# VectorE sums the first half of the value products before it scales the normalised rows; TensorE moves two products between a flip and its use

## The chip, the cores and the metric

One NeuronCore of one Trainium2 chip. The metric is the time of the whole program on the device, in microseconds (us). The engines are TensorE (PE; PEld is its weight load), VectorE (DVE), ScalarE (ACT), GpSimd (POOL) and SyncE (SP, which only issues DMAs). Each runs its own instruction list in order, and they meet at semaphores.

## The reference

2048 rows of 256 values (4 sequences of 512) pass two gated blocks. The first block is the part that the change touches. With `ln` a layer norm:

```python
x = x + tanh(g_xattn[0]) * L0_xattn(ln(x), ctx)      # attention inside a row
x = x + tanh(g_ffn[0])   * L0_ffn(ln(x))             # shared expert + one of 8 experts
x = x + tanh(g_xattn[1]) * L1_xattn(ctx, ctx, ln(x)) # attention over the sequence
x = x + tanh(g_ffn[1])   * L1_ffn(ln(x))             # expand, butterflies, gelu, contract

# L0_xattn, for one row: Q, K, V are 16 heads of 16 values
qk = einsum('ih,jh->ij', Q, K) / 4        # i, j index the 16 values, h the heads
valued = einsum('ij,jh->ih', softmax(qk), V)
out = valued.reshape(256) @ Wo.T
# shared expert
y = (gelu(x @ w1s) * (x @ w2s)) @ w3s
```

Each row attends only to itself, so `qk` and `valued` are 4096 products a row each. They can't be done as matmuls; VectorE and GpSimd do them element by element.

## The kernel before

The first part handles 16 tiles of 128 rows in a software pipeline. A step works on up to five tiles: `t0` (newest) has its keys, values and queries projected, `t1` its scores computed, `t2` its attention finished, `t3` its output projected, normalised and sent into the shared expert, `t4` its shared expert finished. Step number t has `t0 = t`; so tile n is `t1` in step n + 1 and `t3` in step n + 3. Steps 0 to 5 and 16 are written out, steps 6 to 15 run as a loop of two steps (an even and an odd one), and a `drain` finishes the last three tiles. Every engine has its own `step` function, so the order in which each takes the tiles is written by hand.

On VectorE a step starts with `scores` (L1540, 4096 products of queries in PSUM with keys) and `score_sums` (L1549), with `mult` (L1738, the two halves of gelu times up) ahead of each. Then come short ones: `add_attended` (L1559), the layer norm of `t3` (`stats` L1564, `moments` L1569, `guarded` L1574), row maximum and shift of `t1` (L1588, L1597), `guarded_first` (L1582), `exp_sums` (L1605), `shares` (L1621). `normal_rows` (L1615) scales the 128x256 rows of `t3`; it needs the reciprocal root that GpSimd makes from `guarded`. `attended` sums the value products in two halves (L1630, twice) and scales them (L1638). `add_shared` (L1646) adds the shared expert's rows.

GpSimd in a step: `second_root` of `t3` (L552), then for `t1` twice a product of 2048 (L619, in and out of SBUF) and an add of its halves (L621), with `first_root` (L559) between. There is one buffer, PRODV, of two halves:

```python
gp.wait_ge(s["exp_done"], n + 1)
gp.wait_ge(s["kv_sb"], n + 1)
for hf in range(2):
    gp.wait_ge(s["av_read"], 2 * (n - 1) + hf + 1)
```

So the first product of a tile waits until the exponentials are there (ACT L1277) and VectorE has summed the same half of the tile before.

TensorE in a step: flip of the attended rows (PB[3]), `out_rows`, second half of the up products of `t4`, keys and values of `t0` (128x512), its queries (128x256), `down_rows`, flip of the normalised rows, `gate`, first half of the up products of `t3`. Between a flip and its use ScalarE copies the turned rows from PSUM (L1217, L1222). ScalarE also loads its function table again whenever it turns from gelu to exponential and back (ACT_TABLE_LOAD).

SyncE loads tile t + 2 into the buffers of tile t once `kv_done` and `q_done` of tile t are there, after it has stored the normalised rows of `t3` (`keep_rows`).

Of the kernel before, what the change touches and what calls it, by code (L numbers as in the profile page):

```python
# [23 lines left out]
ALU = mybir.AluOpType  # L24
ACT = mybir.ActivationFunctionType
AX = mybir.AxisListType
# [6 lines left out]
NH = 16  # L33
# [21 lines left out]
def build(nc, x, xT, ctxT, gates, wq0, wkv0, wo0, wg, wexp, wk1, wv1, wq1, wo1, bo1,  # L55
          weT, uplow, dnlow, high, cols, wc, bc, db, out):
    with ExitStack() as ctx:
# [323 lines left out]
        def first(jp, n):  # L381
            return isinstance(jp[0], int) and num(jp) < n
# [346 lines left out]
        def _(pe):  # L729
# [30 lines left out]
            def up_half(t3, hf):  # L760

                n = 2 * num(t3) + hf
                for bank, w, done, free in ((PB[6], W1, "h1_done", "gelu_done"),
                                            (PB[7], W2, "h2_done", "mult_done")):
                    if not (first(t3, 1) and hf == 0):
                        pe.wait_ge(s[free], n)
                    for q in range(4):
                        m = 4 * hf + q
                        product(bank[:, q * P:(q + 1) * P], lambda k: w[:, k, m * P:(m + 1) * P],
                                lambda k: X2T[:, t3[1], k, :], KD, s[done] if q == 3 else None)  # L770
# [12 lines left out]
            def out_rows(t3):  # L783

                n3 = num(t3)
                pe.wait_ge(s["aT_sb"], n3 + 1)
                if not first(t3, 1):
                    pe.wait_ge(s["lg_sb"], n3)
                product(PB[5][:, 0:D], lambda k: AT[:, k, :], lambda k: WO0[:, k, :], KD, s["o_done"])
# [9 lines left out]
            def normal_rows(t3):  # L799

                pe.wait_ge(s["xn2_ready"], num(t3) + 1)
                flip(PB[3], XH[:, t3[1], :], s["x2T_done"])
# [6 lines left out]
            def step(of):  # L809
                t0, t3, t4 = of(0), of(3), of(4)  # L810
                if t3 is not None:
                    attended(t3)
                    out_rows(t3)
                if t4 is not None:
                    up_half(t4, 1)
                if t0 is not None and first(t0, 1):
                    warm(PB[0], 8)
                    pe.wait_ge(exact, 2)
                    pe.wait_ge(wq_in, 16)
                    product(PB[5][:, 0:D], lambda k: rounded(ONES[:, :]), lambda k: WQ0[:, k, :], KD,  # L820
                            s["wq_mean"])
                    pe.wait_ge(s["wq_ready"], 1)
                    queries(t0)
                    pe.wait_ge(w_in, 16)
                if t0 is not None:
                    n = num(t0)
                    pe.wait_ge(tile_in[t0[1]], 48 * t0[0] + 48)
                    if not first(t0, 1):
                        pe.wait_ge(s["kv_sb"], n)
                    product(PB[4][:, :], lambda k: CTX[:, t0[1], k, :], lambda k: WKV0[:, k, :], KD,  # L830
                            s["kv_done"])
                    if not first(t0, 1):
                        queries(t0)
                    if first(t0, 2) and not first(t0, 1):
                        pair_products()
                if t4 is not None:
                    down_rows(t4)
                if t3 is not None:
                    normal_rows(t3)
                if t3 is not None:  # L840
                    gate(t3)
                    up_half(t3, 0)
                if t0 is not None and first(t0, 2) and not first(t0, 1):
                    fold_up()
# [6 lines left out]
            def queries(t0):  # L851

                pe.wait_ge(tile_in[t0[1]], 48 * t0[0] + 48)
                if not first(t0, 1):
                    pe.wait_ge(s["qk_prod"], num(t0))
                product(PB[1][:, 0:D], lambda k: XT[t0[1]][:, k, :], lambda k: WQ0[:, k, :], KD, s["q_done"])
# [670 lines left out]
        def _(dve):  # L1527
# [18 lines left out]
            def score_sums(t1):  # L1546

                dve.wait_ge(s["qk_prod"], num(t1) + 1)
                dve.tensor_reduce(SCP.rearrange("p (i j) -> p i j", i=DK),  # L1549
                                  PRODQ[:, :].rearrange("p (i j h) -> p i j h", i=DK, j=DK), AX.X, ALU.add)\  # L1550
                    .then_inc(s["scores"], 1)

            def add_attended(t3):

                n3 = num(t3)
                dve.wait_ge(s["o_done"], n3 + 1)
                if first(t3, 1):
                    dve.wait_ge(tanh_s, 1)
                dve.scalar_tensor_tensor(X[:, n3, :], PB[5][:, 0:D], TG[:, 0:1], X[:, n3, :],  # L1559
                                         ALU.mult, ALU.add).then_inc(s["x1_ready"], 1)  # L1560
# [24 lines left out]
            def row_max(t1):  # L1585

                dve.wait_ge(s["scores"], num(t1) + 1)
                dve.tensor_reduce(SM[:, 0, :], SCP.rearrange("p (i j) -> p i j", i=DK), AX.X, ALU.max)\  # L1588
                    .then_inc(s["rowmax"], 1)
# [28 lines left out]
            def shares(t2):  # L1618

                dve.wait_ge(s["sums"], num(t2) + 1)  # L1620
                dve.reciprocal(RI[:, :], SM[:, 1, :]).then_inc(s["recip"], 1)  # L1621

            def attended(t2):

                n2 = num(t2)
                aov = AOP.rearrange("p (i h) -> p i h", i=DK)
                H2 = NH // 2
                for hf in range(2):
                    dve.wait_ge(s["av_half"], 2 * n2 + hf + 1)
                    dve.tensor_reduce(  # L1630
                        aov[:, :, hf * H2:(hf + 1) * H2],
                        PRODV[:, :].rearrange("p (f i h j) -> p f i h j", f=2, i=DK, h=H2)
                        [:, hf, :, :, 0:DK // 2], AX.X, ALU.add).then_inc(s["av_read"], 1)
                dve.wait_ge(s["av_read"], 2 * n2 + 2)
                dve.wait_ge(s["recip"], n2 + 1)
                if not first(t2, 1):
                    dve.wait_ge(s["aT_done"], n2)
                dve.tensor_tensor(AO[:, :].rearrange("p (i h) -> p i h", i=DK), aov,  # L1638
                                  spread(RI[:, :].rearrange("p (i o) -> p i o", o=1), 2, NH),
                                  ALU.mult).then_inc(s["a_ready"], 1)  # L1640

# [7 lines left out]
            def step(of):  # L1649
                t0, t1, t2, t3, t4 = of(0), of(1), of(2), of(3), of(4)  # L1650
                if t1 is not None:
                    scores(t1)
                if t4 is not None:
                    mult(t4, 0)
                if t1 is not None:
                    score_sums(t1)
                if t4 is not None:
                    mult(t4, 1)
                if t3 is not None:
                    add_attended(t3)  # L1660
                if t3 is not None:
                    hold(s["x1_ready"], num(t3) + 1)
                    stats(t3, 1, "ln2")
                if t1 is not None:
                    row_max(t1)
                if t3 is not None:
                    moments(t3, 1, "ln2")
                if t1 is not None:
                    shift(t1)
                if t3 is not None:  # L1670
                    guarded(t3, 1, "ln2")
                if t0 is not None:
                    guarded_first(t0)
                if t2 is not None:
                    exp_sums(t2)
                    shares(t2)
                if t3 is not None:
                    normal_rows(t3)
                if t2 is not None:
                    attended(t2)  # L1680
                if t4 is not None:
                    add_shared(t4)

            def second_norm(t3):

# [6 lines left out]
            def drain():  # L1692

                a, b, c = tile(T - 3), tile(T - 2), tile(T - 1)
                mult(a, 0)
                second_norm(b)
                exp_sums(c)
                shares(c)
                normal_rows(b)
                mult(a, 1)  # L1700
                attended(c)
                add_shared(a)
                mult(b, 0)
                second_norm(c)
                normal_rows(c)
                mult(b, 1)
                choices()
                add_shared(b)
                places()
                mult(c, 0)  # L1710
                one_hots()
                mult(c, 1)
                expert_of_tiles()
                inverse()
                slots_of_tiles()
                add_shared(c)
# [494 lines left out]
```

## Time and profile before

| | |
|---|---|
| median of 3 runs | 770.26 us (768.25 to 772.27) |
| profiled execution | 768.17 us, span 766.4 us |
| busy share | PE 91%, DVE 79%, POOL 54%, ACT 50% |
| granted TensorE clock, mean | 0.98 |
| first part | about 0 to 297 us |
| the 16 score products on VectorE | first starts 12.3 us, last 257.3 us |

Times in rows are in microseconds from the start of the span unless marked ns. A line number is that of the kernel before. "Idle before" is the time for which the engine stood still ahead of the instruction, with what released it.

### The profile page before, as it was taken

The numbers are of one execution on the slowest core, as the hardware profiler recorded it, in microseconds if no ns is written. First come the engines' busy times: TensorE is split into PE (matmuls) and PEld (weight loads), VectorE is DVE, ScalarE is ACT, GpSimd is POOL, SyncE is SP. The second block draws the span as 40 slices with busy tenths as digits, with TensorE's granted clock in tenths as the row PEclk, the third lists the DMA queues.
The fourth block names the chain that finished last, engine by engine and source line by source line (L and its number), as shares of the span: only waits on it lengthen the run. The fifth ranks groups of instructions, "written<-read, shape, count | busy, mean of one in ns | idle before, by whom it ended". The sixth has DMA issues, their size and how long they took to land.

```text
span 766.4 us, 12694 instructions
## 1 busy us (share of the span) xinstructions
PE 697.5 (91%) x4347; PEld 585.7 (76%) x4347; DVE 607.5 (79%) x910; ACT 380.2 (50%) x682; POOL 416.6 (54%) x304
## 2 busy tenths in 40 slices
PE   6659999999999899889999999999976999999996
PEld 4438888878887788567777777777865999989996
DVE  4789999999999945799978887887787767677653
ACT  2323433433433321366666777666643575555643
POOL 3898888888889880406987666665032101110000
PEclk9959999999999999999999999999998999999999
DMA  9501010011036012232354416000010101000000
GB/s 285 202 28 29 28 29 27 27 34 48 28 97 289 8 62 69 69 138 97 123 193 189 189 29 248 28 22 21 15 36 27 35 21 56 29 28 8 15 15 21
DMA packets 28642, 56.43 MB, mean 74 GB/s; under 512 B 3408, under 2 KB 24656, under 8 KB 27440
## 3 DMA queue, kind: packets, MB, share of 16 engines
q1 hardware_dynamic: 23408, 47.64, 17.4%
q0 software_dynamic: 1872, 5.11, 2.5%
q10 hardware_dynamic: 3312, 3.02, 1.2%
q8 instruction: 30, 0.49, 0.3%
q14 instruction: 20, 0.16, 0.1%
HBM read 48.55 MB, written 7.21 MB: 73 GB/s over the span
## 4 chain that ended last, share of the span: by engine, by line
PE 50%; DVE 19%; POOL 12%; issue 10%; ACT 7%; DMA 1%; DVEq 1%; POOLq 0%; ACTq 0%
PE bank L733 20%; PE bank L742 16%; POOL PRODV L619 8%; PE bank L988 8%; PE bank L750 4%; DVE PRODQ L1540 2%; POOL PRODV L621 2%; DVE SLOT_r L1917 2%; DVE bank L1549 2%; DVE PRODV_r L1917 2%; DVE bank L1630 2%; DVE STC L2005 1%; ACT L1446 1%; ACT XS L1446 1%; ACT L1277 1%
## 5 line engine op out<-in xcount | busy, mean ns | idle before, releaser
L619 POOL TENSOR_TENSOR PRODV<-SHARED 128x2048 f32<-128x2048 f32 x32 | 144.7, 4522 | 28.8 <-DVE bank L1630 25.0
L733 PE MATMUL bank<-ROWS,SLOT 128*128 128x128 f32 x1024 | 122.8, 279 | 0.0
L733 PEld LDWEIGHTS bank<-ROWS,SLOT 128*128 128x128 f32 x1024 | 120.4, 195 | 0.8
L712 POOL TENSOR_TENSOR RS<-VE,MHALF 128x2 f32<-128x2 f32 x16 | 13.1, 819 | 151.1 <-DVE VE L2012 151.1
L733 PE MATMUL bank<-SLOT,XST 128*128 (+1 forms) x184 | 82.9, 593 | 0.5 <-ACT XST L1344 0.5
L621 POOL TENSOR_TENSOR PRODV<-PRODV 128x1024 f32<-128x1024 f32 x32 | 74.7, 2335 | 2.5
L1549 DVE TENSOR_REDUCE bank<-PRODQ 128x256 f32<-128x4096 f32 x16 | 70.7, 4419 | 0.1
L1540 DVE TENSOR_TENSOR PRODQ<-bank,SHARED 128x4096 f32<-128x4096 f32 x16 | 70.6, 4413 | 0.0
L636 POOL DMA_INDIRECT XS<-normal_rows,INV x23 | 27.4, 1192 | 71.2 <-PE bank L750 49.9
L1917 DVE TENSOR_TENSOR PRODQ_r<-SLOT,ROWS_r 128x1024 fp32r<-128x1024 f32 x44 | 63.6, 1446 | 0.0
L733 PE MATMUL bank<-SLOT,HA 128*128 128x256 f32 x256 | 58.3, 381 | 2.4 <-DVE HA L1738 2.4
L1917 DVE TENSOR_TENSOR SHARED_r<-bank,HA_r 128x512 fp32r<-128x512 f32 x46 | 31.5, 686 | 35.8 <-ACT HA_r L1338 35.2
L733 PEld LDWEIGHTS bank<-SLOT,XST 128*128 128x128 f32 x184 | 33.2, 190 | 33.8 <-issue 33.0
L1917 DVE TENSOR_TENSOR W_r<-SLOT,PRODQ_r 128x1024 fp32r<-128x1024 f32 x44 | 57.6, 1308 | 0.0
L1331 ACT ACTIVATE PRODQ_r<-SLOT 128x1024 fp32r (+1 forms) x44 | 46.5, 1057 | 21.1 <-issue 20.6
L733 PEld LDWEIGHTS bank<-SLOT,HA 128*128 128x128 f32 x256 | 48.1, 190 | 9.3 <-DVE HA L1738 2.9
L1354 ACT ACTIVATE ROWS_r<-SLOT 128x1024 fp32r (+1 forms) x46 | 49.2, 1071 | 6.4 <-PE bank L742 6.4
L988 PE MATMUL bank<-W_r,HA_r 128*128 128x256 f32 x176 | 49.6, 282 | 0.0
L988 PE MATMUL bank<-PRODQ_r,SHARED_r 128*128 128x256 f32 x176 | 49.5, 281 | 0.0
L988 PE MATMUL bank<-PRODQ_r,HA_r 128*128 128x256 f32 x176 | 49.5, 281 | 0.0
L742 PE MATMUL bank<-ROWS_r,WORK_r 128*128 128x512 f32 x136 | 48.9, 399 | 0.0
L742 PE MATMUL bank<-SLOT_r,PRODQ_r 128*128 128x256 f32 x256 | 47.6, 286 | 1.4 <-DVE SLOT_r L1917 1.4
(269 smaller groups left out, 1828.1 us busy)
## 6 DMA issues: line engine op xcount, KB each, us to landing
SLOT<-wexp SPq DMA_DIRECT2D x9, 3072.0 KB, 11.5
ROWS<-xT SPq DMA_DIRECT2D x16, 128.0 KB, 2.2
SHARED<-ctxT SPq DMA_DIRECT2D x16, 128.0 KB, 2.4
X<-x SPq DMA_DIRECT2D x16, 128.0 KB, 2.4
normal_rows<-ROWS SPq DMA_DIRECT2D x16, 128.0 KB, 1.7
WET<-ctxT SPq DMA_DIRECT2D x4, 512.0 KB, 8.4
out<-X SPq DMA_DIRECT2D x16, 128.0 KB, 1.7
expert_rows<-YS ACTq DMA_DIRECT2D x12, 128.0 KB, 1.7
```

The costliest lines, as they stand in the source:

```text
L619: gp.tensor_tensor(o, pr, v, ALU.mult).then_inc(s["av_prod"], 1)
L621: gp.tensor_tensor(o[:, :, :, 0:DK // 2], o[:, :, :, 0:DK // 2], o[:, :, :, DK // 2:DK], ALU.add).then_inc(s["av_half"], 1)
L636: gp.indirect_dma_start(out=XS[:, n % 2, :], out_offset=None, in_=xs, in_offset=bass.IndirectOffsetOnAxis(ap=INV[:, n:n + 1], axis=0))\
L733: last = pe.matmul(dst, lhs(k), rhs(k), start=(k == 0), stop=(k == chunks - 1))
L742: last = pe.matmul(dst, f32r(a), f32r(b), start=(k == 0 and n == 0), stop=(k == chunks - 1 and n == 2))
L750: last = pe.transpose(bank[:, k * P:(k + 1) * P], src[:, k * P:(k + 1) * P], IDENT[:, :])
L988: last = pe.matmul(PB[7][:, 0:D], f32r(a[:, k, :]), f32r(b[:, k, :]), start=(k == 0 and i == 0), stop=(k == KF - 1 and i == 2))
L1331: act.activation(f32r(w3h[:, 4 * r:4 * r + 4, :].rearrange("p k d -> p (k d)")), slot_part(held_for[n2], 2 * KD * F + r * 4 * D, 4 * D), A ...
L1354: act.activation(f32r(W2H[:, :, hf * 512:(hf + 1) * 512]), up_part(held_for[n], hf), ACT.Copy)\
L1540: dve.tensor_tensor(PRODQ[:, :].rearrange("p (i j h) -> p i j h", i=DK, j=DK), spread(PB[1][:, 0:D].rearrange("p (i o h) -> p i o h", i=DK ...
L1549: dve.tensor_reduce(SCP.rearrange("p (i j) -> p i j", i=DK), PRODQ[:, :].rearrange("p (i j h) -> p i j h", i=DK, j=DK), AX.X, ALU.add)\
L1917: dve.tensor_tensor(f32r(lo), value, rounded(high), ALU.subtract).then_inc(done, 1)
```

## The change

On VectorE the two sums of value products leave `attended` and become `value_sums(t2, hf)`. The first is put after `guarded(t3)` and ahead of `normal_rows(t3)`, the second right after it. `shares`, `add_shared` and what is left of `attended` (one product) follow in this order. `add_attended` goes ahead of the second `mult`, `guarded_first` ahead of `moments`, and `exp_sums` ahead of `guarded`. In `drain` both sums stand directly before `attended`, where they were.

On TensorE `out_rows` goes behind the second half of the up products, and `queries` goes from behind keys and values to the place between the flip of the normalised rows and `gate`.

```diff
@@ TensorE, step
                 if t3 is not None:
                     attended(t3)
-                    out_rows(t3)
                 if t4 is not None:
                     up_half(t4, 1)
+                if t3 is not None:
+                    out_rows(t3)
...
-                    if not first(t0, 1):
-                        queries(t0)
                     if first(t0, 2) and not first(t0, 1):
                         pair_products()
                 if t4 is not None:
                     down_rows(t4)
                 if t3 is not None:
                     normal_rows(t3)
+                if t0 is not None and not first(t0, 1):
+                    queries(t0)
                 if t3 is not None:
                     gate(t3)
                     up_half(t3, 0)
@@ VectorE
+            def value_sums(t2, hf):
+                H2 = NH // 2
+                dve.wait_ge(s["av_half"], 2 * num(t2) + hf + 1)
+                dve.tensor_reduce(
+                    AOV[:, :, hf * H2:(hf + 1) * H2],
+                    PRODV[:, :].rearrange("p (f i h j) -> p f i h j", f=2, i=DK, h=H2)
+                    [:, hf, :, :, 0:DK // 2], AX.X, ALU.add).then_inc(s["av_read"], 1)
@@ VectorE, step
                 if t1 is not None:
                     score_sums(t1)
+                if t3 is not None:
+                    add_attended(t3)
                 if t4 is not None:
                     mult(t4, 1)
-                if t3 is not None:
-                    add_attended(t3)
                 if t3 is not None:
                     hold(s["x1_ready"], num(t3) + 1)
                     stats(t3, 1, "ln2")
                 if t1 is not None:
                     row_max(t1)
+                if t0 is not None:
+                    guarded_first(t0)
                 if t3 is not None:
                     moments(t3, 1, "ln2")
                 if t1 is not None:
                     shift(t1)
+                if t2 is not None:
+                    exp_sums(t2)
                 if t3 is not None:
                     guarded(t3, 1, "ln2")
-                if t0 is not None:
-                    guarded_first(t0)
                 if t2 is not None:
-                    exp_sums(t2)
-                    shares(t2)
+                    value_sums(t2, 0)
                 if t3 is not None:
                     normal_rows(t3)
                 if t2 is not None:
-                    attended(t2)
+                    value_sums(t2, 1)
+                    shares(t2)
                 if t4 is not None:
                     add_shared(t4)
+                if t2 is not None:
+                    attended(t2)
```

## Rows read from the trace of the kernel before

**Rows 1.** Costliest groups of the page: busy and mean ns, idle before, releaser.
```profile
L619 POOL TENSOR_TENSOR PRODV<-SHARED 128x2048 f32<-128x2048 f32 x32 | 144.7, 4522 | 28.8 <-DVE bank L1630 25.0
```

**Rows 2.** Timeline of POOL, steps 11 and 12: start, us, instruction, idle before.
```profile
186.46 0.54 POOL L552 TENSOR_TENSOR MV<-MV,MHALF 128x1 f32<-128x1 f32 x1
188.84 4.53 POOL L619 TENSOR_TENSOR PRODV<-SHARED 128x2048 f32<-128x2048 f32 x1 [1.84 <-DVE bank L1630]
...
195.75 0.55 POOL L559 TENSOR_TENSOR ROW<-ROW,MHALF 128x1 f32<-128x1 f32 x1
196.27 4.53 POOL L619 TENSOR_TENSOR PRODV<-SHARED 128x2048 f32<-128x2048 f32 x1
...
203.18 0.55 POOL L552 TENSOR_TENSOR MV<-MV,MHALF 128x1 f32<-128x1 f32 x1
205.49 4.54 POOL L619 TENSOR_TENSOR PRODV<-SHARED 128x2048 f32<-128x2048 f32 x1 [1.76 <-DVE bank L1630]
```

**Rows 3.** Timeline of DVE over the same steps.
```profile
187.22 0.41 DVE L1615 TENSOR_SCALAR ROWS<-X,MV 128x256 f32 x1 [0.84 <-POOL MV L552]
...
190.26 0.48 DVE L1646 SCALAR_TENSOR_TENSOR X<-bank,TG,X 128x256 f32 x1
190.66 4.41 DVE L1540 TENSOR_TENSOR PRODQ<-bank,SHARED 128x4096 f32<-128x4096 f32 x1
...
200.51 0.47 DVE L1559 SCALAR_TENSOR_TENSOR X<-bank,TG,X 128x256 f32 x1
201.13 0.43 DVE L1564 BATCH_NORM_STATS2 ST<-X 128x6 f32 x1 [0.15 <-DVE X L1559]
...
202.01 0.43 DVE L1597 TENSOR_TENSOR ROWS<-bank,SM 128x256 f32<-128x256 f32 x1
202.35 0.14 DVE L1574 TENSOR_SCALAR MV<-MV 128x1 f32<-128x1 f32 x1
...
203.86 0.41 DVE L1615 TENSOR_SCALAR ROWS<-X,MV 128x256 f32 x1 [0.69 <-POOL MV L552]
204.19 2.35 DVE L1630 TENSOR_REDUCE bank<-PRODV 128x128 f32<-128x1024 f32 x2
```

**Rows 4.** Groups of DVE instructions by line, 90.57 to 257.33 us (ten steps).
```profile
L1615 DVE TENSOR_SCALAR ROWS<-X,MV 128x256 f32 x10 | 4.1, 413 | 7.1 <-POOL MV L552 7.1
```

**Rows 5.** Timeline of PE over the same steps.
```profile
188.06 0.38 PE L750 MATMUL bank<-IDENT,ROWS 128*128 128x128 f32 x2
188.92 0.61 PE L733 MATMUL bank<-WG,ROWS 128*128 128x8 f32 x4 [0.47 <-ACT ROWS L1222]
...
198.43 1.88 PE L733 MATMUL bank<-W,SHARED 128*128 128x512 f32 x4
...
204.47 0.38 PE L750 MATMUL bank<-IDENT,ROWS 128*128 128x128 f32 x2
```

**Rows 6.** Timeline of ACT over the same steps.
```profile
184.11 0.60 ACT L1263 ACTIVATE SHARED<-bank 128x512 f32<-128x512 f32 x1 [3.07 <-POOL PRODV L619]
...
186.02 0.51 ACT L1277 ACTIVATE SHARED<-ROWS,ROW 128x256 f32<-128x256 f32 x1
...
203.89 0.51 ACT L1277 ACTIVATE SHARED<-ROWS,ROW 128x256 f32<-128x256 f32 x1
```

**Rows 7.** Timeline of step 3, POOL and DVE.
```profile
52.78 0.54 POOL L552 TENSOR_TENSOR MV<-MV,MHALF 128x1 f32<-128x1 f32 x1
...
53.36 0.41 DVE L1615 TENSOR_SCALAR ROWS<-X,MV 128x256 f32<-128x256 f32 x1 [1.90 <-POOL MV L552]
```

**Rows 8.** A POOL instruction of the expert part, from the timeline.
```profile
318.73 2.13 POOL L655 TENSOR_TENSOR WORK<-PRODQ,PRODV 128x1024 f32<-128x1024 f32 x1
```

**Rows 9.** One line's instructions: ns min/median/max, first and last start, forms.
```profile
L1917 DVE TENSOR_TENSOR W_r<-SLOT,ROWS_r x2: 1212/2101/2990, 319.0 to 321.9; 128x1024 fp32r<-128x1024 f32 x2
```

**Rows 10.** The same view of the two casts of L1909.
```profile
L1909 DVE CAST WK_r<-WQ x1: 414/414/414, 360.2 to 360.2; 128x512 fp32r<-128x512 f32 x1
L1909 DVE CAST WO_r<-WV x1: 859/859/859, 370.7 to 370.7; 128x512 fp32r<-128x512 f32 x1
```

More of the change, by code:

```diff
@@ L1621, in shares @@
                 dve.reciprocal(RI[:, :], SM[:, 1, :]).then_inc(s["recip"], 1)
+            AOV = AOP.rearrange("p (i h) -> p i h", i=DK)
+            def value_sums(t2, hf):
[5 more added lines that the diff above has]
+                    [:, hf, :, :, 0:DK // 2], AX.X, ALU.add).then_inc(s["av_read"], 1)
             def attended(t2):
                 n2 = num(t2)
[L1626 to L1633, printed above, removed]
                 dve.wait_ge(s["av_read"], 2 * n2 + 2)
@@ L1637, in attended @@
                     dve.wait_ge(s["aT_done"], n2)
-                dve.tensor_tensor(AO[:, :].rearrange("p (i h) -> p i h", i=DK), aov,
+                dve.tensor_tensor(AO[:, :].rearrange("p (i h) -> p i h", i=DK), AOV,
                                   spread(RI[:, :].rearrange("p (i o) -> p i o", o=1), 2, NH),
@@ L1700, in drain @@
                 mult(a, 1)
+                value_sums(c, 0)
+                value_sums(c, 1)
                 attended(c)
```

## The prediction

> **What bounds the kernel now.** I read the page first, for the costliest groups and who releases whom, then the timelines of POOL, DVE, PE and ACT over one even and one odd step of the loop, to find which loop of waits closes. The page shows that GpSimd's product of 2048 is the largest group and stood 25.0 us waiting for VectorE's sum of the value products [rows 1]. The timeline of POOL shows the loop. A step takes 205.49 - 188.84 = 16.65 us; from the score product of step 12 (190.66) to that of step 16 (257.3, in the table above) it is 66.6 / 4 = 16.66, and I use 16.67. Of it GpSimd works 203.18 + 0.55 - 188.84 = 14.89 and stands 1.76 to 1.84 [rows 2]. In that gap VectorE, which has waited 0.7 us a step for GpSimd's root [rows 4], scales the rows, sums the first half, and lets GpSimd go: 203.18 to 203.86, 204.19, 205.49 [rows 2, 3]. Though the first half of the products has been ready for 7 us, its sum stands behind an instruction that waits for GpSimd's last piece of work. PE is next: flip to flip is 16.41 us, with two stalls of 0.47 for ScalarE's copies [rows 5]. So three engines lie close: POOL 14.89, DVE 16.67 - 0.71 = 15.96, PE 16.41 - 0.94 = 15.5.
>
> **The change, VectorE.** Same instructions, another order. What shortens the list:
> - the wait for the root, 0.71 a step, if the root now comes while the first sum runs;
> - `stats` 0.62 after `add_attended`, where the next instruction could start 0.40 later, as after L1646 [rows 3]; the second mult goes between: 0.22;
> - three more waits of an instruction for the one before it (sum to reciprocal, maximum to shift, sums to scaling) get other work between; I take 0.1 each, an estimate from instructions of 256 elements, which start 0.34 apart where nothing is waited for [rows 3]. Bounds 0 and 0.45.
>
> VectorE's own loop comes to 16.67 - 0.71 - 0.22 - 0.3 = 15.44; I use 15.4.
>
> **The change, TensorE.** Each flip now has work behind it. The flip to gate distance of 0.86 [rows 5] shrinks to what two transposes take, about 0.25 (an estimate; bounds 0 and the modelled 0.38), so PE's list is 16.41 - 2 x 0.61 = 15.2, plus some 0.2 where the up products now reach the bank before the gelu has read it. `down_rows` waits for the second mult, which stands 0.4 later on VectorE; in return PE has one product less ahead. PE follows at VectorE's pace. `queries` come later, about 5 us before the next score product on the old clock and 0.3 before it on the new; slack, but little. What is moved past on SyncE's queue: loading tile t + 2 waits for these queries, some 1.5 us later, and is used a whole step later: nothing. In step 1 the pair products no longer stand behind queries that wait for VectorE, so the first exponentials come some 0.3 us earlier. In the drain PE waits 0.3 longer for the later mult of step 16. Both are estimates; they cancel.
>
> If nothing else happened: 11 steps x (16.67 - 15.4) = 14 us less.
>
> **What GpSimd now collides with.** In the kernel before, `normal_rows` (L1615) always runs while GpSimd stands still, because GpSimd's next product waits for the sum behind it [rows 2, 3]. After the change that product can start at the same moment. Does it matter? Three rows say that it does. A VectorE instruction with two SBUF inputs that takes 1.21 us took 2.99 when it started 0.3 us behind GpSimd's product of 2.13 [rows 8, 9]: it did nothing until GpSimd was through. Of two equal casts, SBUF to SBUF, one took 0.41 and one, beside GpSimd, 0.86 [rows 10]. And L1615 seems to be of the same kind as the cast: the cast does 512 elements in 0.41 us where L1597 needs 0.43 for 256, a double pace. L1615 does 256 elements with two per-row scalars in 0.41, while instructions of 256 with one such scalar take 0.47 to 0.48 at the single pace (L1559, L1646) [rows 3, 4, 10]. So it seems to run at the double pace too and, I take it, holds what GpSimd needs. The Trainium skill ("SBUF — State Buffer", Who interferes with whom) says that VectorE in a two-port mode and GpSimd hold one port pair for the whole instruction, and the second to issue blocks. By that rule the trace agrees, and the forecast below holds; without it the time would be that of the third case.
>
> The price: if GpSimd's product (4.53 us) starts first, L1615 and all behind it come up to 4.5 us late. If L1615 starts first, GpSimd loses 0.4, which it has.
>
> **Who is first.** Offsets from the start of the score product S, loop of 15.4.
> - From the shift (L1597) to the next S: 0.34 + 0.33 (sums), 0.06 (guarded), 1.13 (half of L1630), 0.33 (L1615), 1.13, 0.17 (reciprocal, estimate), 0.40, 0.34 = 4.2. So the shift is at 11.2, the first value sum at 11.9, L1615 could start at 13.0.
> - The value sum releases GpSimd 1.30 after its start (204.19 to 205.49): 13.2.
> - Even steps: the table load waits for the shift; exponentials start 1.88 after it and last 0.51 [rows 3, 6]. GpSimd's product starts at 11.2 + 1.88 + 0.51 + 0.08 = 13.65, so L1615 is first.
> - From this product to the next root are 203.18 - 188.84 = 14.34. In the following, odd, step the root starts at 13.65 + 14.34 - 15.4 = 12.6. In odd steps L1615 follows it by 187.22 - 186.46 = 0.76: 13.35. Exponentials: PE ended keys and values at 198.43 + 1.88 - 190.66 = 9.65; now `down_rows` stands directly behind them and waits for the second mult until 10.4, so they end at 10.4 to 10.6. Their copy is followed by the exponentials in 1.91 (184.11 to 186.02, the table load in between doesn't wait for the shift) [rows 6], done by 13.1. So GpSimd's product starts at 13.2, ahead of L1615 by 0.15 to 0.2. It collides: L1615 starts when the product ends, at 17.7, 4.6 later than it could, and the step lasts 20.0.
> - After it GpSimd is early, the even step is clean (15.4), and the next odd one has the same 13.65 behind it. It repeats: steps 7, 9, 11, 13, 15. Step 5 is written out, where the root is followed in 0.58, as in rows 7; it comes out just in time.
> - Step 3: GpSimd's root is last of all (52.78). A product follows a root in 0.52 (195.75 to 196.27), L1615 in 0.58 [rows 2, 7]. L1615 had waited 1.90 there, which is room for the 1.30 of the first sum, so nothing else holds GpSimd. It collides too, and PE stands behind it: +4.5, less 0.6 for PE's saved stalls: +3.9.
>
> **Sum.** +3.9 - 11 x 1.27 + 5 x 4.6 = 3.9 - 14.0 + 23.0 = +13, on the profiled 768.17 gives 781; the median shown lies 2.1 higher, and 770.26 + 13.2 = 783.5. Own range 779 to 788: loop 15.3 to 15.6, and the collision 4.4 to 4.7.
>
> **Rivals.**
> - *The odd steps are just in time, step 3 collides.* Should VectorE's tail behind the shift take 4.4 and not 4.2, the root is early enough. A step then takes about 15.55 (L1615 waits for the root): 3.9 - 11 x 1.12 = -8.4, 762. For it: every offset is good to 0.1 and the margin is 0.2. Against: a later exponential in the loop pushes the other way.
> - *No collision at all*: L1615 doesn't share with GpSimd, or wins in step 3 too. -12.3, 758. For it: no row shows L1615 beside a long GpSimd instruction. It decides from L1615 staying at 0.41 us.
> - *PE takes the wait*: mult, `down_rows`, flip and queries close a loop at 16.4 to 16.7. Then 768 to 770. Against it: 15.2 to 15.4 of work and 0.3 of slack at each crossing.
>
> **Chances.** Forecast 0.56; just in time 0.23; no collision 0.15; PE 0.06. The range takes in both signs: 757.5 to 788 leaves out about 0.15. Three runs differ by 0.5%, so 0.5% (3.9 us) is about what can be told: faster 0.39, same 0.04, slower 0.57.
>
> **What will show it.** L1615 (its new line) at 4 to 5 us in step 3 and in odd steps, with GpSimd's product running over it; even steps of 15.4 and odd ones of 20. POOL's wait for L1630 gone or 0.3. PE's stalls for L1217 and L1222 gone. If L1615 is 0.41 throughout and steps are 15.4 to 15.6, the second or third case holds. Wrong would be my offsets, if the first value sum starts more than 0.2 us earlier or later against the root than worked out.

## The result and the profile after

| | before | after |
|---|---|---|
| median | 769.31 us (4 runs, 768.25 to 772.27) | 792.43 us (4 runs, 790.45 to 793.83) |
| profiled execution | 768.17, span 766.4 | 792.09, span 790.3 |
| granted TensorE clock, mean | 0.98 | 0.955 |
| last of the 16 score products starts | 257.33 | 277.91 |
| last scaling of rows starts | 293.76 | 316.28 |

The ratio is 1.0278, with a 95% interval of 1.0258 to 1.0297: 23 us slower. The forecast was 783.5 us, slower, with an own range of 779 to 788. The direction and the collision that it named are there; the time lies above the range. The new line numbers of the changed kernel are L1541 (score products), L1616 (scaling of the rows), L1642 and L1650 (`attended`, `add_shared`), L1218 and L1223 (ScalarE's two copies) and L1278 (exponentials); L552, L619 and L1630 keep theirs.

The page of the changed kernel: the clock in 40 slices, and costliest groups.

```profile
PEclk9859998989898989989999999999999999999999
...
L619 POOL TENSOR_TENSOR PRODV<-SHARED 128x2048 f32<-128x2048 f32 x32 | 144.2, 4507 | 11.8 <-ACT SHARED L1278 10.1
...
L750 PE MATMUL bank<-IDENT,ROWS 128*128 128x128 f32 x64 | 14.4, 311 | 38.4 <-DVE ROWS L1616 31.0
```

What the change was to do it did: GpSimd's products, which stood 28.8 us, 25.0 of them for VectorE's sum [rows 1], now stand 11.8, of which 10.1 for the exponentials. The new entry is TensorE's: 31.0 us of waiting for the scaled rows, where it was 5.9 before, all in step 3. Of the 31.0, step 3 has 11.3 and five later steps 3.94 each. The view of that one line (ns min/median/max, first and last start, who waited for it):

```profile
L1616 DVE TENSOR_SCALAR ROWS<-X,MV x16: 400/408/4599, 53.4 to 316.3; 128x256 f32 x10, 128x256 f32<-128x256 f32 x6
its engine sat idle before it (us, times) until:
  POOL MV L552: 3.8, 7
who waited for it (us, times):
  PEld bank L750: 34.0, 6
  PE bank L750: 31.0, 6
```

Before, each of these took 0.41 us [rows 4]. Now ten do and six take 4.48 to 4.60: those that start at 53.41, 120.78, 158.19, 195.73, 233.27 and 270.83, in steps 3, 7, 9, 11, 13 and 15, the very ones that the forecast named. One clean odd step and one with a collision, from the timeline (start, us, instruction, idle before):

```profile
89.01 0.56 POOL L552 TENSOR_TENSOR MV<-MV,MHALF 128x1 f32<-128x1 f32 x1
89.68 0.40 DVE L1616 TENSOR_SCALAR ROWS<-X,MV 128x256 f32<-128x256 f32 x1
89.93 4.52 POOL L619 TENSOR_TENSOR PRODV<-SHARED 128x2048 f32<-128x2048 f32 x1 [0.36 <-DVE bank L1630]
...
157.42 0.55 POOL L552 TENSOR_TENSOR MV<-MV,MHALF 128x1 f32<-128x1 f32 x1
157.49 0.51 ACT L1278 ACTIVATE SHARED<-ROWS,ROW 128x256 f32<-128x256 f32 x1
158.16 4.48 POOL L619 TENSOR_TENSOR PRODV<-SHARED 128x2048 f32<-128x2048 f32 x1 [0.19 <-ACT SHARED L1278]
158.19 4.60 DVE L1616 TENSOR_SCALAR ROWS<-X,MV 128x256 f32 x1 [0.42 <-POOL MV L552]
162.71 1.22 DVE L1630 TENSOR_REDUCE bank<-PRODV 128x128 f32<-128x1024 f32 x1
...
162.85 0.69 PE L750 MATMUL bank<-IDENT,ROWS 128*128 128x128 f32 x2 [3.94 <-DVE ROWS L1616]
...
163.33 1.92 PE L733 MATMUL bank<-W,ROWS 128*128 128x256 f32 x4
...
165.75 5.33 PE L733 MATMUL bank<-ROWS,SLOT 128*128 128x128 f32 x32
```

In step 5 the scaling starts 0.25 us ahead of the product, and both run at their usual length. In step 9 the product is 0.03 ahead, and the scaling ends just behind it (162.79, against 158.16 + 4.48 = 162.64). TensorE, which waits for these rows, stands 3.94 us. Then comes what the forecast lacks: its work behind that wait is slow. The flip takes 0.69 (0.38 in [rows 5]), four products of 256 columns 1.92, 32 up products 5.33. Here are whole stretches of the changed kernel, with the granted clock in the column before the DMA share (steps 5 and 6, then 9 and 10, then the 6 us behind the collision):

```profile
76.79:92.03 15.24, 15.20 (x102) 13.23 (x101) 15.21 (x19) 6.81 (x13) 14.72 (x7) 1.00 0.12 36
92.03:107.27 15.24, 15.19 (x102) 13.26 (x101) 15.24 (x19) 6.89 (x13) 14.18 (x7) 1.00 0.12 35
144.80:165.28 20.48, 16.50 (x101) 14.00 (x101) 19.49 (x18) 6.81 (x13) 20.05 (x9) 0.92 0.09 26
165.28:182.34 17.06, 17.02 (x102) 15.15 (x102) 15.40 (x19) 6.87 (x13) 9.34 (x5) 0.89 0.10 31
162.70:168.70 6.00, 5.85 (x24) 5.50 (x25) 5.43 (x6) 0.56 (x2) 5.98 (x3) 0.50 0.29 87
```

Clean steps take 15.24, and TensorE is busy for 15.20 of them: it has no slack in which a lower clock could hide. A step with a collision takes 20.48, and the clean even step behind it 17.06: TensorE comes back from its wait at a granted clock of 0.50, which is 1.2 GHz, and keeps it for some 6 us, across the border of the steps.

### The profile page after: what moved, and what is told of

It is laid out like the page before. It is cut to its first block, busy times and chain, and to the rows that moved or that the text cites. A ratio compares the mean times of both kernels' runs of the same rounds, so it can differ in the third digit from the quotient of the medians.

```text
span 790.3 us, 12694 instructions
## 1 busy us (share of the span) xinstructions
PE 708.6 (90%) x4347; PEld 597.1 (76%) x4347; DVE 627.3 (79%) x910; ACT 380.2 (48%) x682; POOL 416.8 (53%) x304
## 4 chain that ended last, share of the span: by engine, by line
PE 51%; DVE 19%; POOL 11%; issue 8%; ACT 6%; DMA 2%; SPq 1%; DVEq 0%; POOLq 0%; ACTq 0%
PE bank L733 22%; PE bank L742 16%; PE bank L989 8%; POOL PRODV L619 8%; PE bank L750 4%; DVE ROWS L1616 4%; DVE bank L1550 3%; POOL PRODV L621 2%; DVE SLOT_r L1927 2%; DVE PRODV_r L1927 2%; DVE STC L2015 1%; ACT L1447 1%; ACT XS L1447 1%; DMA COLS<-cols 1%; ACT L1278 1%
## 5 line engine op out<-in xcount | busy, mean ns | idle before, releaser
L619 POOL TENSOR_TENSOR PRODV<-SHARED 128x2048 f32<-128x2048 f32 x32 | 144.2, 4507 | 11.8 <-ACT SHARED L1278 10.1
L733 PE MATMUL bank<-ROWS,SLOT 128*128 128x128 f32 x1024 | 130.2, 289 | 0.4
L733 PEld LDWEIGHTS bank<-ROWS,SLOT 128*128 128x128 f32 x1024 | 125.9, 204 | 2.9 <-ACT G L1214 2.8
L712 POOL TENSOR_TENSOR RS<-VE,MHALF 128x2 f32<-128x2 f32 x16 | 13.1, 819 | 150.4 <-DVE VE L2022 150.4
L733 PE MATMUL bank<-SLOT,XST 128*128 (+1 forms) x184 | 85.2, 607 | 0.5 <-ACT XST L1345 0.5
L1541 DVE TENSOR_TENSOR PRODQ<-bank,SHARED 128x4096 f32<-128x4096 f32 x16 | 70.8, 4424 | 6.0 <-PE bank L733 5.8
L750 PE MATMUL bank<-IDENT,ROWS 128*128 128x128 f32 x64 | 14.4, 311 | 38.4 <-DVE ROWS L1616 31.0
```

The lines of the kernel that those rows point to most:

```text
L619: gp.tensor_tensor(o, pr, v, ALU.mult).then_inc(s["av_prod"], 1)
L733: last = pe.matmul(dst, lhs(k), rhs(k), start=(k == 0), stop=(k == chunks - 1))
L750: last = pe.transpose(bank[:, k * P:(k + 1) * P], src[:, k * P:(k + 1) * P], IDENT[:, :])
L1541: dve.tensor_tensor(PRODQ[:, :].rearrange("p (i j h) -> p i j h", i=DK, j=DK), spread(PB[1][:, 0:D].rearrange("p (i o h) -> p i o h", i=DK ...
```

## The experiments

All are versions of the changed kernel, except where the one before is named. Each ratio is to the kernel before in the same job, with its 95% interval.

| kernel | median us | ratio | score product to score product, us |
|---|---|---|---|
| changed | 792.43 | 1.0278 [1.0258, 1.0297] | 20.48 and 17.06 |
| e1, rows before product | 756.71 | 0.9804 [0.9781, 0.9828] | 15.7 mean |
| e6, scaling with one SBUF input | 757.34 | 0.9808 [0.9777, 0.9839] | 15.7 mean |
| e4, product in two pieces | 770.77 | 0.9995 [0.9973, 1.0016] | 17.76 and 15.24 |
| e5, 32 fillers | 793.45 | 1.0278 [1.0247, 1.0309] | 22.38 and 15.24 |
| e7, 16 fillers | 778.69 | 1.0094 [1.0061, 1.0128] | 19.88 and 15.23 |
| e9, one copy ahead of the exponentials | 777.83 | 1.0077 [1.0049, 1.0105] | mixed |
| e10, two copies | 759.38 | 0.9846 [0.9819, 0.9873] | 15.8 and 15.24 |
| e2, before + TensorE's order | 767.49 | 0.9943 [0.9914, 0.9972] | 16.67 |
| e3, before + VectorE's order | 770.43 | 0.9988 [0.9975, 1.0002] | 16.4 |
| e8, e3 + rows before product | 769.01 | 0.9967 [0.9941, 0.9992] | 16.4 |

**e1: the product may not overtake the rows.** Ahead of its first product GpSimd also waits for the scaled rows. Nothing else is changed.

```diff
                     gp.wait_ge(s["exp_done"], n + 1)
                     gp.wait_ge(s["kv_sb"], n + 1)
+                    if t3 is not None:
+                        gp.wait_ge(s["xn2_ready"], num(t3) + 1)
                     for hf in range(2):
```

> The changed kernel, but GpSimd waits for xn2_ready of t3 before its first product of 2048, so normal_rows always goes first. Port theory: none of the sixteen normal_rows lasts over 0.45 us, TensorE never waits 4 us, its clock stays at the full level from step 5 to 16, and a step takes 15.5 to 15.7 us, set by the loop product, root, normal_rows, product (14.34 + 0.77 + 0.41 + 0.1). Total 757 to 760. Rival, the long instruction has a cause of its own (the reading of X, a store to DRAM): it stays at 4.5 us in the same steps and the total stays near 790. Rival, the order of the change is itself slower: no long instruction, yet over 770.

Measured 756.71, a hair under the expected range, with steps of 15.7. A wait more makes the kernel 36 us faster than the changed one, and 2% faster than the one before. Both rivals of the expectation are out: the instruction still reads and stores the same rows and is short all 16 times, and the total is far below 770. The same line:

```profile
L1618 DVE TENSOR_SCALAR ROWS<-X,MV x16: 403/414/415, 54.3 to 284.7; 128x256 f32 x10, 128x256 f32<-128x256 f32 x6
```

**e6: the scaling in another form.** e1 shows that the order matters, not what the two share. Here the order is left free. The rows are scaled as x*r - mean*r, with mean*r in a column of PSUM and spread over the row, so the instruction has one tensor input in SBUF; it takes 0.48 us, as L1646 does [rows 3]. It costs one small instruction and one wait more.

```diff
-                dve.tensor_scalar(XH[:, t3[1], :], X[:, n3, :], MV[:, 1, 0:1], MV[:, 1, 3:4],
-                                  ALU.subtract, ALU.mult).then_inc(s["xn2_ready"], 1)
+                dve.tensor_scalar(PB[3][:, D:D + 1], MV[:, 1, 0:1], MV[:, 1, 3:4], None, ALU.mult)\
+                    .then_inc(iotaf, 1)
+                dve.wait_ge(iotaf, n3 + 5)
+                dve.scalar_tensor_tensor(XH[:, t3[1], :], X[:, n3, :], MV[:, 1, 3:4],
+                                         spread(PB[3][:, D:D + 1], 1, D),
+                                         ALU.mult, ALU.subtract).then_inc(s["xn2_ready"], 1)
```

> The changed kernel, but normal_rows computes x * r - mean * r with one SBUF tensor and a PSUM column (a tiny product for mean * r ahead of it), at the pace of one element a cycle; GpSimd isn't held. Port theory: the instruction takes 0.45 to 0.5 us in every step, also where GpSimd's product of 2048 is already running, because with one SBUF input at the single pace it shares nothing; no collision, total 757 to 761, steps 15.3 to 15.6. Rival, any VectorE instruction on these rows is held by a running GpSimd product: 4.5 us again in steps 3, 7, 9 and so on, total 790 or more.

Measured 757.34, with steps of 15.7 on average, a little above the 15.3 to 15.6 expected. In steps 3, 7, 9, 11, 13 and 15 GpSimd's product goes first, by 0.33 to 0.44 us, and the scaling runs inside it, undisturbed; in steps 4, 5 and 16 the two start within 0.01 us of each other. The scaling takes 0.48 all 16 times (timeline of step 9, then the line):

```profile
148.72 4.53 POOL L619 TENSOR_TENSOR PRODV<-SHARED 128x2048 f32<-128x2048 f32 x1
148.88 0.22 DVE L1616 TENSOR_SCALAR bank<-MV 128x1 f32<-128x1 f32 x1 [0.26 <-POOL MV L552]
149.14 0.48 DVE L1619 SCALAR_TENSOR_TENSOR ROWS<-X,MV,bank 128x256 f32<-128x256 f32 x1
```
```profile
L1619 DVE SCALAR_TENSOR_TENSOR ROWS<-X,MV,bank x16: 479/481/483, 54.2 to 284.3; 128x256 f32<-128x256 f32 x16
```

So no semaphore or queue holds the scaling up: it is its own form against a running GpSimd instruction. What the two share no trace shows; that the form decides, this run does. The form with the lower time alone (0.41 against 0.48) is the one that can cost 4.6. The Trainium skill ("SBUF — State Buffer", Who interferes with whom) says that a VectorE instruction with at most one SBUF input outside the two-port modes doesn't contend with GpSimd; by that rule the trace agrees, at 0.48 beside the product.

**e4: a shorter product.** GpSimd's first product of 2048 becomes two of 1024; the second may slip behind the scaling. Same arithmetic.

```diff
+                        if hf == 0:
+                            for h in range(2):
+                                at = slice(h * (DK // 2), (h + 1) * (DK // 2))
+                                ins = gp.tensor_tensor(o[:, at], pr[:, at], v[:, at], ALU.mult)
...
```

> The changed kernel, with GpSimd's first product of 2048 issued as two of 1024. Port theory: normal_rows is held for one instruction only, so 2.2 to 2.5 us in place of 4.5 in the steps that collide. TensorE then waits 1.8 and not 3.9; if its clock stays up, an odd step takes 18.1 and an even one 15.3, total 772 to 777; if it falls all the same, 779 to 783. The 0.1 us that the second instruction costs GpSimd makes the root later, so the same steps collide. Rival, a fixed penalty for colliding: still 4.5 us.

Measured 770.77, a little under the expected range of 772 to 777. The block lasts as long as the instruction that was there first, not as long as GpSimd's work:

```profile
153.57 4.69 POOL L622 TENSOR_TENSOR PRODV<-SHARED 128x1024 f32<-128x1024 f32 x2
153.82 2.23 DVE L1623 TENSOR_SCALAR ROWS<-X,MV 128x256 f32 x1 [0.69 <-POOL MV L552]
156.10 0.20 PEld L757 LDWEIGHTS bank<-IDENT,ROWS 128*128 128x128 f32 x2 [2.24 <-DVE ROWS L1623]
156.10 0.44 PE L757 MATMUL bank<-IDENT,ROWS 128*128 128x128 f32 x2 [1.84 <-DVE ROWS L1623]
```

TensorE stands 1.84 instead of 3.94 and its clock holds: the flip takes 0.44, and the even step is 15.24 again, at a granted clock of 1.00 (steps 9 and 10, the columns as in the stretches above):

```profile
140.16:157.92 17.76, 15.88 (x106) 13.64 (x106) 17.07 (x19) 6.85 (x14) 17.60 (x9) 1.00 0.10 30
157.92:173.16 15.24, 14.99 (x99) 12.78 (x97) 15.24 (x20) 6.83 (x13) 12.16 (x7) 1.00 0.13 34
```

Halving the block took off 21.7 us (792.43 - 770.77), more than six times 2.3.

**e5 and e7: TensorE kept busy through the block.** Is it really the clock that makes the even steps long? In the odd steps from 7 on TensorE multiplies something useless between `down_rows` and the flip of the rows, into a bank that is overwritten later: 32 matmuls in e5, 16 in e7.

```diff
                     down_rows(t4)
+                if t0 is not None and t0[1] == 1 and not first(t0, 6):
+                    warm(PB[3], 16)
```

> The changed kernel, with 32 extra transposing-size matmuls (128x128 on the identity, into a bank that is rewritten) ahead of the flip of the normalised rows in the odd steps 7 to 15; about 3.7 us, the time for which TensorE otherwise waits. Clock theory (what the forecast missed): the granted clock stays at its full level, the even step behind a collision takes 15.2 to 15.4 in place of 17.05 and the odd one about 19.9 in place of 20.5; five pairs save 2.0 to 2.4 each, total 780 to 783. Rival, the even step is long because GpSimd or ScalarE has got out of phase: no change, 792.

Measured 793.45, where 780 to 783 was expected. The even steps fell from 17.06 to 15.24 as expected, but the 32 matmuls show as 64 records and take 7.31 us, not the 3.7 reckoned; that is longer than the block, and the odd steps grew to 22.38. So half of them:

> As the kernel with the filling products, but with 16 of them and not 32. The 32 had shown as 64 passes of 7.3 us and not as the 3.7 meant: the even step behind a collision fell from 17.05 to 15.23 us as the clock theory has it, and the odd step, now waiting for the filler, grew by as much, so that the total stayed. With 16 (3.65 us) the filler ends with the wait it stands in. Clock theory: even step 15.2 to 15.3, odd step 19.6 to 20.5, five pairs save 1.8 to 2.6 each: total 779 to 784. Rival, that the total can't fall because something else sets the pair: 792.

Measured 778.69, 0.3 under the range expected from the clock; both steps are inside theirs. The block itself is as long as before (start 155.13), the work behind it is fast:

```profile
154.95 4.49 POOL L619 TENSOR_TENSOR PRODV<-SHARED 128x2048 f32<-128x2048 f32 x1
155.13 4.46 DVE L1618 TENSOR_SCALAR ROWS<-X,MV 128x256 f32 x1 [0.57 <-POOL MV L552]
...
159.65 0.44 PE L750 MATMUL bank<-IDENT,ROWS 128*128 128x128 f32 x2 [0.38 <-DVE ROWS L1618]
...
159.92 1.03 PE L733 MATMUL bank<-W,ROWS 128*128 128x256 f32 x4
...
161.15 3.82 PE L733 MATMUL bank<-ROWS,SLOT 128*128 128x128 f32 x32
```

The four products of the queries fall from 1.92 to 1.03, the up products from 5.33 to 3.82, the odd step from 20.48 to 19.88 and the even one from 17.06 to 15.23. Useless matmuls gain 13.7 us (792.43 - 778.69). Most of it is what the low clock costs in steps 7 to 16: a pair of steps falls from 37.54 to 35.11, and five pairs at 2.43 would be 12.1 (an estimate, with step 16 taken like the other even steps).

**e2, e3 and e8: the two halves of the change.** e2 is the kernel before with TensorE's new order alone, e3 with VectorE's alone, e8 is e3 with the wait of e1.

> The kernel before with TensorE's part of the change alone. The loop of GpSimd's product, root, normal_rows, first sum is untouched at 16.65 us, and normal_rows still runs while GpSimd stands: steps 16.6 to 16.7, total 768 to 772 (the queries of steps 1 and 3 come later, up to 2 us). If TensorE's order itself costs something, over 775; if it had been the bound, 765 or less.

> VectorE's part of the change alone, TensorE in the order of before. TensorE's list with its two stalls is 16.4 us, so it sets the step, and the root comes 1 us earlier against normal_rows than with both parts. By my reckoning of who goes first (13.65 + 14.34 - 16.4 = 11.6, against 12.4 as the latest start of a harmless root) no odd step of the loop collides, step 3 alone does: steps 16.4, total 767 to 772. Rival, the new order of VectorE collides whatever the pace: 785 to 795.

> As the kernel in which GpSimd lets normal_rows go first, but TensorE in the order of before. No collision at all; TensorE's list of 16.4 sets the step: total 765 to 768, against 757 with TensorE's new order. If it comes out at 757 too, TensorE's part of the change is worth nothing.

Measured 767.49, 770.43 and 769.01: the first a little under what was expected, the second inside it, the last a little above. In e2 the loop is the old one, 16.67 a step, and the scaling takes 0.413 us on average. In e3 it is 16.4, which is TensorE's old flip to flip time [rows 5]: VectorE got its shorter list, and TensorE's set the pace: VectorE now stands about a microsecond a step for `down_rows`.

```profile
177.94 0.48 DVE L1649 SCALAR_TENSOR_TENSOR X<-bank,TG,X 128x256 f32 x1 [1.02 <-PE bank L733]
```

One scaling of 16 collides there, in step 3 (4.56 us); in the slower loop the product of the odd steps starts 0.9 to 1.0 us behind the scaling. With no collisions, as in e8 and e1, VectorE's order alone gives 769.01 and both together 756.71. Each half is worth next to nothing alone, since the other engine is close behind, and both together 12 us more.

**e9 and e10: who comes first.** By the forecast it is a race of tenths of a microsecond between the scaling and the product. The product waits for the exponentials. So ScalarE gets useless work in the odd steps from 7 on, which delays the product a little:

```diff
+                if t0 is not None and t0[1] == 1 and not first(t0, 6):
+                    act.activation(PICK[:, 0:P], IDENT[:, :], ACT.Copy)
                 if t1 is not None:
...
                     act.activation(PR[:, t1[1], :], SC[:, :], ACT.Exp, scale=ROW1[:, t1[1], 3:4])\
```

> The changed kernel with one small useless piece of work added: in odd steps from step 7 on ScalarE copies 128x128 into a scratch before its exponentials (some 0.25 us, an estimate from its 0.38 for 256 elements in the changed kernel), so these steps' exponentials, and with them GpSimd's first product, come some 0.25 us later. In the changed kernel that product started 0.03 us before the scaling of the rows (158.16 against 158.19). Theory (who starts first decides): in steps 7 to 15 the scaling now starts first and takes 0.41 us instead of 4.6, each pair of steps falls from 37.5 to 31 or 32 us, step 3 still collides, and the total is 758 to 766 us although work was added. Rival (GpSimd and VectorE get into each other's way whoever starts first, or something else makes these steps long): the scaling stays at 4 to 5 us and the total is 792 or more.

Measured 777.83, between the two ranges. The copy was 0.30 us, and the margin that it left is not the same in every step: in steps 7, 11 and 15 the product starts 0.02 to 0.03 behind the scaling, in 9 and 13 0.14 behind. The scaling takes 4.64, 4.64 and 4.65 us in the first three, and 0.41 in the other two. Steps 9 and 10 together took 30.94 us (144.75 to 175.69) and not 37.54. Steps 7 and 13, from the timeline:

```profile
120.65 4.64 DVE L1618 TENSOR_SCALAR ROWS<-X,MV 128x256 f32 x1 [0.57 <-POOL MV L552]
120.67 4.48 POOL L619 TENSOR_TENSOR PRODV<-SHARED 128x2048 f32<-128x2048 f32 x1 [0.23 <-ACT SHARED L1280]
...
226.58 0.41 DVE L1618 TENSOR_SCALAR ROWS<-X,MV 128x256 f32 x1 [0.44 <-POOL MV L552]
226.72 4.65 POOL L619 TENSOR_TENSOR PRODV<-SHARED 128x2048 f32<-128x2048 f32 x1 [0.35 <-ACT SHARED L1280]
```

The clock follows the collisions here too. Step 8 has one ahead of it (in step 7), step 10 has none; the work in both is the same:

```profile
127.78:144.75 16.97, 16.93 (x102) 15.07 (x102) 15.40 (x19) 6.87 (x13) 9.33 (x5) 0.90 0.10 31
160.44:175.69 15.25, 15.01 (x99) 12.80 (x97) 15.25 (x20) 6.84 (x13) 14.28 (x7) 1.00 0.11 34
```

e10 has a second copy, into the next 128 columns.

> The changed kernel with two useless copies of 128x128 on ScalarE instead of one, in the odd steps from step 7 on, ahead of the exponentials. With one copy (0.30 us) GpSimd's first product started 0.14 us behind the scaling of the rows in steps 9 and 13, which then took 0.41 us, and 0.02 to 0.03 behind it in steps 7, 11 and 15, where the scaling still took 4.64. Theory (who comes first decides, with a margin of between 0.03 and 0.14 us): another 0.3 us of work puts the product 0.3 to 0.45 behind the scaling in all five steps; each pair of steps then takes 31.0 to 31.6 us, only step 3 collides, and the total is 758 to 764 us. Rival (the outcome of a near tie is not set by the order): some of the five still take 4.6 us, 6.6 us each of them in the total, 768 us or more.

Measured 759.38, inside the range. All five products now start 0.20 to 0.26 us behind the scaling (0.3 to 0.45 was expected), all five scalings take 0.41, and only step 3 still collides:

```profile
L1619 DVE TENSOR_SCALAR ROWS<-X,MV x16: 405/412/4553, 54.4 to 286.4; 128x256 f32 x10, 128x256 f32<-128x256 f32 x6
```

Two useless copies a pair of steps gain 33 us against the changed kernel: the order at that one point decides.

## Why the direction was right and the size wrong

The forecast's mechanism is what the runs show; its price of a collision left out the clock.

**GpSimd's wait and VectorE's list: right.** The clean steps 5 and 6 took 15.24 (forecast 15.4), and e1 with no collision 756.71 (the third case said 758).

**Form and price of the collision itself: right.** The scaling takes 4.48 to 4.60. At a full clock (e7) a step with a collision is 19.88 - 15.24 = 4.64 longer than a clean one, with 4.6 in the sum and 4.4 to 4.7 as its bounds. That the scaling gets in GpSimd's way by its form was inferred from its pace, and e6 bears it out. One row said less than was read from it: of the two casts [rows 10] the short one had a GpSimd instruction open beside it as well (359.23 to 360.93, which ended behind the cast; the long cast's ran from 369.67 to 371.29 and ended ahead of it). They differ in which of the two engines was through first, and not in whether GpSimd had work.

**Which steps: right, on a margin smaller than worked out.** In step 9 the root starts 12.62 after the score product (forecast 12.6), the scaling could start at 13.39 (13.35). The product started at 13.36, not at 13.2: the exponentials ended at 13.20, later than the 13.1 reckoned, and were what it waited for, not the sum. The margin was 0.03 us, not 0.15 to 0.2; in step 7 it was 0.14. That the forecast held in spite of it is partly luck, since 0.14 the other way frees the scaling (e9). The chance of 0.23 for the just-in-time case was not too high.

**The failed step: "After it GpSimd is early, the even step is clean (15.4)".** It is free of a collision but not of its consequences. TensorE's wait in the collision was counted as time, and not as what it does to the clock behind it, which went down to 0.50. The even steps took 17.06, and 0.6 of the odd ones' 20.48 (against 20.0) is the clock too, by e7. From the start of the score product in step 5 to that in step 16 the forecast had 11 x 15.4 + 23.0 = 192.4 us; measured are 201.1 (277.91 - 76.79): four even steps at +1.65 make 6.6, five odd ones at +0.48 make 2.4, and the clean steps 5 and 6 give back 0.3.

**The smaller terms.** Step 3 and what follows it came to +2.85 at the start of step 5's score product (76.79 against 73.94), forecast +3.9. Behind the last score product 3.3 us more were lost (23.9 in the span less 20.58). Up to the last scaling of rows it is 1.9 (38.37 against 36.43), of which 1.6 goes with step 16's low clock, as e7, without it, takes 36.77. A collision isn't needed for that: e1 has none and takes 38.47 there, with a low clock from 258.0 to 261.4 us, begun 1.4 us after TensorE came back from a wait of 2.19 for VectorE's mult. The other 1.4 lie behind the last scaling, where all twelve kernels have the same code and their profiled executions take anything from 471.4 to 475.5 us (472.6 before, 474.0 after): that is scatter and no cost of the change. Together: 12.9 forecast, + 8.7 - 1.05 + 3.3 = 23.9, which is the growth of the span. One slip is in the forecast's own sum: its terms make 12.9 and it adds 13.2 to the median, so 783.5 should read 783.2; that changes nothing.

## What to carry to other kernels

Before an instruction is moved ahead of its neighbour, ask what ran beside the neighbour until now: a wait that looks wasteful may be what keeps a short VectorE instruction of this form apart from a long GpSimd one. Where two such instructions race, fix the order with a semaphore (e1) or take the form that isn't held up (e6), as a margin of tenths of a microsecond is decided by work on a third engine. And price a TensorE wait twice: once as time, and once by whether the clock is still high behind it.

## What the runs showed of the hardware that was not expected

- A near tie goes to GpSimd: with its product starting 0.02 to 0.03 us behind the scaling in the trace, the scaling still took 4.64 us; at 0.14 behind it took 0.41, and then the product itself took 4.65 instead of 4.52.
- A TensorE wait of 3.94 us was followed by some 6 us at a granted clock of 0.50, in each of five steps; a wait of 1.84 us by none (e4: clock 1.00, 15.24 for the next step). The length of the wait alone doesn't decide it: in step 16 TensorE waits 2.0 to 2.4 us for the second mult, and in e1, e2, e4, e6 and e10 a low clock of 3.4 us came with it, but not in e7 (2.19) or the kernel before (2.37).
- Cutting GpSimd's instruction in two cuts the block in two (4.6 to 2.23 us) and makes GpSimd's work only 0.17 us longer (4.69 us for both pieces, 4.52 for one).
